# Convolution and relation passes of a graph network: ScalarE copies each slot sum out of PSUM, VectorE adds the copy

## The reference

```python
# convolution: 64 features, messages weighted by an edge filter and a cosine cutoff
h = (x @ W_node_to_message.T) @ W_lin1.T
m = h[src] * ((rbf @ W_radial_to_message.T) * C[:, None])
agg = segment_sum(m, dst)
# relation: 8 edge types, 256 features, mean over the incoming edges
msg = einsum('nd,rde->rne', h, weight)[edge_type, src]
m = segment_sum(msg, dst) / max(degree, 1)
```

## Time and profile before

| | |
|---|---|
| median of 3 runs | 9026.64 us (9007.27 to 9045.2) |
| span of the profiled execution | 9513.5 us |
| convolution pass, in the trace | 4155 to 5568 us |
| relation pass, in the trace | 6250 to 7516 us |
| attention passes, in the trace | 449 to 1901 and 2329 to 3693 us |
| busy over the span | PE 64%, POOL 54%, DVE 52%, PEld 43%, ACT 19% |

### The profile page before, as it was taken

One profiled execution on the slowest core, in us unless ns is written; L12 is line 12 of the kernel. 1 busy time (PEld: TensorE's weight loads), 2 busy tenths in 40 slices (PEclk: granted clock), 3 DMA queues, 4 the chain that ended last, 5 costly groups with the idle time before them and its releaser, 6 DMA issues. The chain is left out here.

```text
span 9513.5 us, 114282 instructions
## 1 busy us (share of the span) xinstructions
PE 6103.6 (64%) x21566; PEld 4079.9 (43%) x21567; DVE 4907.6 (52%) x10800; ACT 1764.1 (19%) x5802; POOL 5094.9 (54%) x4638
## 2 busy tenths in 40 slices
PE   4557777766777775746555578955555566666660
PEld 2245555544555553545555543423222344343430
DVE  4256677765777777753333332133333554444447
ACT  0223333312333331210000001100000122222221
POOL 0057677601777773036666610047666468888880
PEclk7666777668777776755555558976666788888885
DMA  1463333313333332221111123433232346666665
GB/s 28 149 176 102 98 103 106 99 33 125 107 106 104 106 107 57 60 67 24 23 24 23 24 52 122 138 96 89 88 88 88 102 55 68 68 69 69 68 69 168
DMA packets 556641, 796.06 MB, mean 84 GB/s; under 512 B 97181, under 2 KB 430798, under 8 KB 555215
## 3 DMA queue, kind: packets, MB, share of 16 engines
q0 software_dynamic: 271168, 487.56, 25.4%
q1 hardware_dynamic: 258318, 280.98, 9.7%
q10 hardware_dynamic: 27092, 26.85, 1.1%
HBM read 543.23 MB, written 251.81 MB: 84 GB/s over the span
## 5 line engine op out<-in xcount | busy, mean ns | idle before, releaser
L588 POOL DMA_INDIRECT at_x<-table,at_idx x1680 | 1922.6, 1144 | 643.6 <-issue 525.9
L2211 POOL DMA_INDIRECT acc<-sc_rows,sc_idx x832 | 1353.2, 1626 | 298.4 <-DMA acc<-sc_rows,sc_idx 186.6
L660 PE MATMUL at_psO<-at_x,at_main 128*128 128x273 f32 x3328 | 1322.5, 546 | 3.4 <-issue 2.1
L1626 POOL DMA_INDIRECT conv_x<-conv_table,conv_idx x840 | 844.1, 1005 | 515.2 <-DVE conv_prod L1718 276.0
L1679 PE MATMUL rel_psO<-rel_x,rel_hot 128*128 128x257 f32 x1664 | 653.1, 534 | 616.4 <-issue 375.6
L1626 POOL DMA_INDIRECT rel_x<-rel_table,rel_idx x840 | 836.1, 995 | 392.7 <-issue 222.4
L718 ACT COPY at_sums<-at_psO 128x273 f32<-128x273 f32 x1664 | 629.3, 388 | 1804.9 <-PE at_psO L660 1194.8
L660 PEld LDWEIGHTS at_psO<-at_x,at_main 128*128 128x128 f32 x3328 | 798.4, 260 | 254.2 <-issue 61.1
L2251 PE MATMUL sc_psR<-gated,sc_pick 128*128 x1664 | 597.0, 456 | 448.2 <-ACTq L2289 444.6
L1679 PE MATMUL conv_psO<-conv_msg,conv_hot 128*128 128x64 f32 x1664 | 448.4, 433 | 581.6 <-issue 373.1
L826 DVE TENSOR_TENSOR agg<-agg,at_sums 128x273 f32 x1664 | 733.6, 441 | 43.9 <-DVE agg L826 3.8
(11 more groups left out here) (397 smaller groups left out, 9098.7 us busy)
## 6 DMA issues: line engine op xcount, KB each, us to landing
at_place<-places SPq DMA_DIRECT2D x212, 256.0 KB
rel_table<-rt_rows SPq DMA_DIRECT2D x50, 1024.0 KB
at_x<-table,at_idx POOLq DMA_INDIRECT x1680
acc<-zeros ACTq DMA_DIRECT2D x4, 6553.5 KB
la_t<-acc SPq DMA_DIRECT2D x40, 642.5 KB
conv_attr<-in_attr_T SPq DMA_DIRECT2D x840, 6.0 KB
conv_x<-conv_table,conv_idx POOLq DMA_INDIRECT x840
rel_x<-rel_table,rel_idx POOLq DMA_INDIRECT x840
```

The source lines that it names most:

```text
L588: pool.indirect_dma_start(x[b][:, j, 0:TABW], None, d.table[0:NR, :], bass.IndirectOffsetOnAxis(ap=idx[b][:, j:j + 1], axis=0)).then_inc(x ...
L660: nc.tensor.matmul(psO[j % BANKS][:, 0:AGG], main[b % 2][:, j, :], x[b][:, j, 0:AGG], start=True, stop=True).then_inc(o_ready, 1)
L1626: pool.indirect_dma_start(x[b][:, j, 0:WIDE], None, table, bass.IndirectOffsetOnAxis(ap=idx[b][:, j:j + 1], axis=0)).then_inc(x_ready[b], 16)
L2211: pool.indirect_dma_start(d.acc[k][0:NR + P, :], bass.IndirectOffsetOnAxis(ap=idx[b][:, j:j + 1], axis=0), rows[b % 2][:, j, :], None, com ...
```

## The change

A ScalarE stream is added to `phase_sum_messages`. For each slot it waits for the sum (`o_ready`), waits until the add of 16 slots before is done (`acc_done`, which now starts at 16), and copies the sum from its PSUM bank into `out[b % 2]`, an SBUF tile for eight slots of which there are two. The copy raises `copied`. TensorE now waits for `copied` instead of `acc_done` before it reuses a bank. VectorE's add waits for `copied` and reads the tile `out` in place of the PSUM bank. The number of banks (four), all shapes, and the order of the instructions of the other engines stay.

```diff
+    copied = sem("sums_copied")
...
+        out = [sb(f"out{b}", [P, GROUP, K]) for b in range(2)]
...
-                    pe.wait_ge(acc_done, i + 1)
+                    pe.wait_ge(copied, i + 1)
...
+            @block.scalar
+            def _(act):
+                act.sem_inc(copied, BANKS)
+
+                def copy_sums(g, b, j):
+                    i = g * GROUP + j
+                    act.wait_ge(o_ready, i + 1)
+
+                    act.wait_ge(acc_done, i + 1)
+                    nc.scalar.copy(out[b % 2][:, j, :], psO[j % BANKS][:, 0:K]).then_inc(copied, 1)
+                with act.Fori(0, NTURN) as it:
+                    for b in range(SETS):
+                        for j in range(GROUP):
+                            copy_sums(it * SETS + b, b, j)
...
-                dve.sem_inc(acc_done, BANKS)
+                dve.sem_inc(acc_done, 2 * GROUP)
...
-                    dve.wait_ge(o_ready, i + 1)
-
-                    dve.wait_ge(acc_done, i + BANKS)
+                    dve.wait_ge(copied, i + 1 + BANKS)
+
+                    dve.wait_ge(acc_done, i + 2 * GROUP)
...
-                    nc.vector.tensor_tensor(to, to, psO[j % BANKS][:, 0:K], ALU.add).then_inc(acc_done, 1)
+                    nc.vector.tensor_tensor(to, to, out[b % 2][:, j, :], ALU.add).then_inc(acc_done, 1)
...
-                dve.wait_ge(acc_done, S + BANKS)
+                dve.wait_ge(acc_done, S + 2 * GROUP)
```

## The result

The changed kernel takes 9053.8 us (median of 20 runs, 9026.23 to 9082.73), the kernel before in the same runs 9038.05 us (median of 20, 8991.0 to 9059.1). The ratio is 1.0025, interval 1.0014 to 1.0037: 23 us slower (13 to 33), where +24 us was forecast. (The two medians are 16 us apart, which lies within this interval.)

The account below looks back on a forecast made before the run. POOL's gathers, 10.0 us a group, were taken to bound both passes. Copies +1, waits 0, add duration 0 and held gathers +23 gave +24 us on 9026.64, 9050 us; own range 9007 to 9072, wider range 8840 to 9120.

Parts of the forecast that it names:

- The bound: Both passes: POOL's gathers, 10.0 us a group, set the pace; 429 us of profiled waits likely belong to the recording.
- The copies and the hop: ScalarE's 832 added copies a pass cost only one more hop's latency at each pass's end: +1 us.
- The waits: TensorE waits for the copy instead of the add; no gain where POOL bounds: 0 to -2 us, taken 0.
- The add from SBUF: VectorE's adds keep their duration, but with two SBUF inputs they hold POOL's gathers: +23 us.
- upper bound: Both passes: any gather whose reading moment falls on an add is held for half of it: 77 us.
- the limit: How long an add must have run when a gather starts in order to hold it: about 0.07 us.
- something for adds in a row: Allowance for successive adds holding gathers, included in taking 23 us rather than the worked-out 17.
- The waits go: Rival: slow stretches occur in timed runs and decoupling cures them, saving up to 429 us; chance 0.24.
- Held one-hots: Rival: shifted VectorE one-hots hold more gathers in both passes, 60 us more, at worst 121; chance 0.26.

Follow-up runs that it names:

- copy_psum_add: Changed kernel, but VectorE's add reads the PSUM bank again and TensorE waits for the add; ScalarE's copies stay: ratio 1.0003 to the kernel before.
- the halves: Changed kernel with the one-hot's row of numbers in PSUM, each relation add made as two of 128 and 129 columns: ratio 0.9972, uncut 0.9971.
- the extra SBUF work: Kernel before with one-hot numbers in PSUM, plus three 500-column VectorE additions a group in the relation pass, both inputs SBUF: 0.9978; one input PSUM: 0.9956.
- before_again: The kernel before, unchanged, run and profiled a second time: ratio 1.001, profiled span 9046.0 us.
- conv_only: The change in the convolution pass alone, the relation pass as in the kernel before: ratio 0.9992.
- rel_only: The change in the relation pass alone, the convolution pass as in the kernel before: ratio 1.0037.

## Why the prediction was right, point by point

**The bound.** Right, and it was the step that mattered. The inference rested on one comparison: a profiled execution 487 us longer than the timed ones, and 429 us of waits that no rate in the pass accounted for. The second profile of before shows both gone. What those stretches were stays open: they were in one recorded execution and in none of the thirteen later profiles, and no run here brought them back.

**The copies and the hop.** Right at next to nothing (1 us said): copy_psum_add, 1.0003 (0.999 to 1.0016). The copies took 373 ns (taken: 374) and, of 64 columns, 212 ns (taken: 245).

**The waits.** Right at nothing. TensorE's 302.4 us of waits for adds were real waits and off the path, and in the changed kernel TensorE waits 322.1 us for the messages in their place: it can run no further ahead than the order of VectorE's work lets it, as the prediction said of the one-hot matrix.

**The add from SBUF.** Right in kind and nearly in size. Worked out 17 us, taken 23, with 77 as the upper bound; measured 21.5 us held by the relation's adds in the change, 21.7 and 21.8 in two more kernels, of which up to 3 us are the noise of the count; with the one-hots out of the way 18.4 and 19.3 us. In the convolution pass under 1 us was said and 3.1 us counted. The step that was off is the limit: the prediction took 0.07 us from a few pairs, and the traces show 0.04. In its own window, 0.07 to 0.30 us, the adds of the change held 17.7 us, the 17 worked out; adds that had run for 0.04 to 0.07 us held 1.8 us more. For whole adds the error is small, for the halves it is most of the miss (5 said, 14.8 counted). What the sum added to the 17, "something for adds in a row", no run shows by itself.

**The page of the skill.** The Trainium skill, page "SBUF — State Buffer", section "Who interferes with whom", says that a VectorE instruction with two SBUF inputs contends with a GpSimd instruction that reads SBUF and one with a single SBUF input does not. By this rule the trace agrees: the relation gather's mean is 976 ns beside the extra SBUF work and 949 ns beside the same work from PSUM. That every gather which meets an add is held, the prediction's +77 us, doesn't come out: 21.5 us in the relation pass and 3.1 in the convolution pass.

**The rivals.** "The waits go" is refuted by before_again and copy_psum_add. "Held one-hots" went the other way by a little: with the change they hold 9.7 us less in the convolution (the same in conv_only) and 8.3 us less in the relation pass, where the spread between traces of one pass is 4. So the changed kernel's trace, from first to last gather, shows the relation pass 1116.6 us long against 1105.5, and the convolution pass 1086.6 against 1095.4: +11 and -9 us, hardly a loss, while the timed runs say +13 to +33. So the sum's +24 beside the measured +23 is in part luck: its interval is 20 us wide, and the sum has no term for the one-hots' gain.

What may fill the gap of some 20 us is TensorE's clock. The twelve runs of rel_only had a mean granted clock of 0.721, the 35 of before beside them 0.726, conv_only 0.726 and copy_psum_add 0.725. Among the runs of one kernel a clock lower by 0.001 goes with some 2 us more; this is an estimate, the slope of straight lines through the runs of every kernel. By it 9 of the 29 us between the means of rel_only and before (the ratio gives 33) go with the clock, and about 19 are left, the 18 by which its traced relation pass was longer. The changed kernel's 20 runs had 0.723. The clocks of the runs before beside them are not on record; the three sets of before that have them show 0.726 to 0.728, which would make 7 to 11 us of the 23. Why the clock was lower, and whether it is the change's doing, stays open.

**What the forecast said would show it.** Copies and adds of the durations named: yes. The relation gather's mean up from 995 ns by 20 to 70: by the letter yes, 1016, but against the second profile's 1005 it is 11, since the one-hots hold less. The convolution gather's mean up by under 20: it fell by 10, for the same reason. Of POOL's waits the forecast said that they would either fall with the time, or stay with the time unmoved. Neither came: they are gone from both kernels' later profiles, and the time did not fall. By these signs alone the run could not have been read; the second profile of before was needed. Gathers of 1.0 to 1.2 us beside adds: yes.

## What to carry to other kernels

Before moving an operand from PSUM to SBUF, look whether the engine that reads it already reads another one from SBUF, and whether GpSimd issues gathers that bound the pass: the instruction gets no longer, and the gathers do. Where such a pass is found, the cheap gain is the other way round: put a constant operand of the longest VectorE instruction into a free PSUM bank (here 57 us for two passes and 117 us for four, of which some 12 us go with a higher clock, 0.734 against 0.728, by the estimate above). And where a profiled execution is 5% longer than the timed ones, profile again before you explain its waits.

## What was not expected of the hardware

A gather is held until 0.13 or 0.14 us before the end of the VectorE instruction in all examples shown (1.49, 1.14, 1.13, 1.20 and 1.05 us), and in the median of the 147 adds counted above, as if it read once, about 0.13 us after its start. Which of the two gives way is decided within a few hundredths of a us: an add that had run for less than 0.04 us was itself longer (0.49 us in place of 0.43), an older one held the gather. Cutting an instruction in two did not free the gathers in proportion (19.3 to 14.8 us held). Freed gathers meet the next instruction: without attention's one-hots, which had held 128.3 us, the scans held 81.4 us instead of 49.5, and POOL's copies took 18 us more.
